# A narrow attention: the output chain of a batch one place forward in the steps, and the fill pieces one step sooner

## The chip, the cores and the metric

The kernel runs on one core of a Trainium2 chip. The metric is the device time of one execution in microseconds (us). The core has five engines that run their own instruction streams and meet only at semaphores: PE (matrix products and transpositions into PSUM), DVE (vector), ACT (activation functions and copies), POOL (general) and SP (issues transfers). Each stream runs in its written order: an instruction that waits holds up everything behind it on its engine.

## The reference, cut to what matters

Two decoder layers over `x` of 4 batches x 256 tokens x 128 channels. The change touches only the attention and the routing inside the third block ("C" in the names):

```python
# _L0_ffn_ref: attention with 16 heads of 8 channels, then a mixture of experts
q, k, v = split(h @ Wq + bq), split(h @ Wk + bk), split(h @ Wv + bv)
att = jnp.einsum('bhqd,bhkd->bhqk', q, k) / jnp.sqrt(jnp.float32(hd))
att = jax.nn.softmax(jnp.where(causal, att, -jnp.inf), axis=-1)
y = jnp.einsum('bhqk,bhkd->bhqd', att, v)
x = x + y.transpose(0, 2, 1, 3).reshape(B, T, D) @ Wp + bp
# experts: layer norm, gate logits, the two best of 8 experts for each token, weights by softmax
logits = flat @ gate_W + gate_b
top_v, top_i = jax.lax.top_k(logits, TOP_K)
mid = gelu(flat @ exp_W1[e] + exp_b1[e]); y_e = mid @ exp_W2[e] + exp_b2[e]
```

Ahead of it stand a wide self-attention (A) and a cross-attention (B) of 16 heads of 64 channels; behind it a second small attention (D), a gated product (E) and a feed-forward block (F).

## The kernel before, in words

All engines walk one list of steps written out by hand. Blocks A and B are the *wide* steps. The **narrow attention** of block C runs in steps `s` of its own (`narrow_step(s)`), from s = -3 on, of which the first few lie inside the last wide steps. A step handles one group of 4 of the 16 heads of one batch: 4 batches x 4 groups = 16 groups (`NGR`), group g = s. What a step does with a group is spread over three steps (CT = 1):

- step s: PE computes the scores of group s (L900) into the 4 banks of `ring`, after a mask product (L834) into each bank; DVE takes the row maxima (L1340, L1341, two of each, `narrow_maxima`); ACT the 8 exponentials (L639, L640), which free the banks.
- step s+1: PE transposes the probabilities in three pieces into the two banks of `ptb` (L828: pieces 0 and 1, and, behind the tail extras and the masks of the next scores, piece 2, which waits for DVE's first copy); DVE copies pieces 0 and 1 (L1377 x2), ACT piece 2 (L648).
- step s+2: PE multiplies with the values (L923, "PV"); ACT copies the product (L655).
- step s+3: PE transposes it back ("tr", L931, into `misc`); DVE divides by the sums (L1355, L1358) into `oN`.

Around this stand **extras** of a batch b, put into the lists `c_head[s]` (PE does them right after the scores, ACT ahead of the exponentials), `c_tail[s]` (PE: behind pieces 0 and 1; ACT: at the end of its step) and `c_dve[s]`. All of them, and tr, share the one PSUM bank `misc`: each use waits until the one before it has been read out (`misc_free`). They are QK and V (projections of a batch), CX (transposition of a later batch), and the *output chain* of a batch, after its last group: **OT** (transposition of `oN`, L855; evicted by ACT, L617), **OUT** (projection, L859; DVE adds bias and residual and takes layer norm statistics, L1383 to L1393; POOL the inverse deviation, L1705, L1706), **hat** (normalised rows, DVE, L1367), **X2** (their transposition, L867; ACT, L622), **GATE** (gate logits, L871; ACT, L628; then `pick` on DVE, L1223 to L1235, the two best experts), **RANK** (running counts of the picked experts, L875 to L885; ACT, L626; then `place` on DVE, L1241 to L1246, POOL's scatter of the rows to memory, and for the second batch of a half `tile_list`, L1251 to L1267). With the list SP loads the rows of the half (`tokens`).

When the scores end (group 15 in step 15) the experts begin. Their pieces stand in one list, `ORDER`: "mid:u" (PE: transposition of a tile of tokens, L954, and first product, L999; ACT: eviction L681 and gelu L688), "out:u" (second product, L1011; DVE L1439) and "put:u" (POOL scatter). `FILL` says how many of its pieces are done after each of the narrow steps 16 to 22; the rest follows after the last narrow step. The 15 tiles of the first half of the batches come first; the tokens of the second half need RANK of batch 3.

Of the kernel before, what the change touches and what calls it, by code (L numbers as in the profile page):

```python
# [32 lines left out]
P = 128  # L33
# [6 lines left out]
FILL = [(16, 1), (17, 2), (18, 2), (19, 5), (20, 6), (21, 6), (22, 3)]  # L40
# [52 lines left out]
def decoder(nc, t):  # L93
    ctx = ExitStack()
    with ctx:
# [413 lines left out]
        with nc.Block() as block:  # L509
# [83 lines left out]
            def _(act):  # L593
# [37 lines left out]
                def narrow_step(s):  # L631
                    from_narrow(c_head[s])
                    if 0 <= s < NGR:
                        if s >= PR:
                            act.wait_ge(c_pt_done, TU * (s - PR + 1))
                        for r in range(G):
                            if r % 2 == 0:
                                act.wait_ge(c_max, 2 * s + r // 2 + 1)
                            nc.scalar.activation(pr[:, s % PR, r, 0:P], ring[:, r, 0:P], ACT.Exp, bias=nmax[:, s, r:r + 1], scale=-1.0)  # L639
                            nc.scalar.activation(pr[:, s % PR, r, P:SW], ring[:, r, P:SW], ACT.Exp, bias=nmax[:, s, G + r:G + r + 1],  # L640
                                                 scale=-1.0).then_inc(c_ring_free, 1)
                    if CT <= s < NGR + CT:
# [13 lines left out]
                    from_narrow(c_tail[s])  # L656
# [536 lines left out]
            def _(dve):  # L1193
# [149 lines left out]
                def narrow_step(s):  # L1343
                    if s:
                        narrow_maxima(s)
                    for kind, b in c_head[s]:
                        if kind == "RANK":
                            place(b, misc_at[kind, b] + 1)
                    if 0 <= s - CT - 2 < NGR:
                        g = s - CT - 2  # L1350
                        b, q = g // NG, g % NG
                        prod4 = misc[:, 0:S].rearrange("p (c h v) -> p c h v", c=CB, v=VW)
                        rs = nrs[:, g, :].rearrange("p (c h) -> p c h", c=CB)
                        dve.wait_ge(misc_done, misc_at["tr", g] + 1)
                        c_ch.step(nc.vector.reciprocal(rs, prod4[:, :, :, HD]))  # L1355
                        if b >= 2 and q == 0:
                            dve.wait_ge(misc_done, misc_at["OT", b - 2] + 1)
                        nc.vector.tensor_tensor(oN[:, b % 2, :, :].rearrange("p c (h j d) -> p c h j d", j=G, d=HD)[:, :, :, q, :],  # L1358
                                                prod4[:, :, :, 0:HD], rs.unsqueeze(3).broadcast_to([P, CB, G, HD]), ALU.mult)\
                            .then_inc(misc_free, 1)  # L1360
                    for kind, b in c_dve[s]:
                        dve.wait_ge(c_rstd, b + 1)
                        if b >= 2:
                            dve.wait_ge(scattered[0], 16 * 2 * HT)
                        for c in range(CB):
                            n = 4 * (b % 2) + 2 * c
                            ins = nc.vector.tensor_scalar(hat[:, n:n + 2, 0:D], x1[:, b % 2, c, :].unsqueeze(1).broadcast_to([P, 2, D]), lmv2[:, b, c, 0:1], lrs2[:, b, c:c + 1],  # L1367
                                                          ALU.subtract, ALU.mult)
                        ins.then_inc(c_xhat, 1)
                    if CT <= s < NGR + CT:  # L1370
                        g = s - CT
                        if g >= 2:
                            dve.wait_ge(c_o_done, g - 1)
                        for u, dst in enumerate((prT[g % 2][:, :, 0, 0:P], prT[g % 2][:, 0:2, :, P:S].rearrange("p h k q -> p (h k) q"))):
                            n = TU * g + u
                            dve.wait_ge(c_pt_done, n + 1)
                            nc.vector.tensor_copy(dst, ptb[:, n % 2, :].rearrange("p (h q) -> p h q", q=P)).then_inc(c_pt_free, 1)  # L1377
                    for e in c_tail[s]:
                        kind, b = e
                        if kind == "OUT":  # L1380
# [13 lines left out]
                    for kind, b in c_head[s]:  # L1394
                        if kind == "GATE":
                            pick(b, misc_at[kind, b] + 1)
                        elif kind == "RANK" and b % 2:
                            tile_list(b // 2)
# [239 lines left out]
            def _(pool):  # L1638
# [54 lines left out]
                def narrow_step(s):  # L1693
# [8 lines left out]
                    for kind, b in c_tail[s]:  # L1702
# [149 lines left out]
```

## Time and profile before

| what | value |
|---|---|
| median of 3 runs | 649.35 us (644.24 to 649.8) |
| the profiled execution | 648.76 us |
| its span, first to last instruction | 647.0 us |
| mean granted clock of TensorE | 0.976 |
| busy: PE, DVE, ACT, POOL | 592.8, 453.6, 397.8, 199.7 us |
| narrow steps 6 to 15, maxima of step 6 to maxima of step 15 | 394.47 to 446.49 us |

All times below are of the profiled execution, counted from the start of its span. A row of the timeline gives the start, the length, the engine, the line, the operation, and in brackets how long the engine had been idle and what ended that. The rows themselves stand in a section further down.

### The profile page before, as it was taken

How to read it: one execution, taken by the hardware profiler on the slowest of the kernel's cores; microseconds unless marked ns; L12 is line 12 of the kernel's file. 1: busy time of each engine (PE TensorE's matmuls, PEld its weight loads, DVE VectorE, ACT ScalarE, POOL GpSimd, SP SyncE). 2: the span in 40 equal slices, each digit the busy share in tenths (PEclk: the TensorE clock that was granted, in tenths of full speed). 3: DMA queues.
4: the chain of work that ended last, by engine and by line, in shares of the span. 5: the costliest groups of instructions: out<-in, count | busy, mean ns of one | idle time of the engine just before them, and what ended most of it. 6: DMA issues, size and time to landing. Idle time of an engine off the chain costs nothing.

```text
span 647.0 us, 12136 instructions
## 1 busy us (share of the span) xinstructions
PE 592.8 (92%) x4082; PEld 416.4 (64%) x4082; DVE 453.6 (70%) x1343; ACT 397.8 (61%) x1234; POOL 199.7 (31%) x265
## 2 busy tenths in 40 slices
PE   5999999999999999999998899887797985899996
PEld 3667776776776766767666466565787974445543
DVE  1989787677788988999988677878332366683402
ACT  3776557777678787777676467775566762144420
POOL 1133030131442442363414523243156545101101
PEclk9999999999999999999999899999699998699999
DMA  9300990000000000000000000193544801000000
GB/s 291 124 2 13 276 59 0 2 1 2 2 1 2 2 0 2 1 2 2 1 2 2 1 2 1 50 397 121 184 164 118 305 32 49 1 0 2 16 0 18
DMA packets 39662, 36.33 MB, mean 56 GB/s; under 512 B 12496, under 2 KB 34640, under 8 KB 39216
## 3 DMA queue, kind: packets, MB, share of 16 engines
q1 hardware_dynamic: 37840, 32.33, 18.3%
q0 software_dynamic: 1472, 3.05, 1.4%
q8 instruction: 34, 0.56, 0.4%
q14 instruction: 28, 0.23, 0.1%
q10 hardware_dynamic: 288, 0.16, 0.1%
HBM read 26.39 MB, written 9.14 MB: 55 GB/s over the span
## 4 chain that ended last, share of the span: by engine, by line
PE 67%; DVE 19%; ACT 8%; issue 3%; DMA 1%; SPq 1%; POOL 0%; POOLq 0%; DVEq 0%; ACTq 0%
PE ring L1029 8%; PE ring L1078 8%; PE obank L1105 8%; PE ptb L1093 6%; PE obank L1113 5%; PE misc L1148 4%; ACT arena L755 3%; PE misc L1056 3%; DVE arena L1518 3%; PE ring L999 3%; PE ptb L1011 3%; PE misc L1057 2%; PE ring L1019 2%; DVE arena L1535 2%; DVE arena L1341 2%
## 5 line engine op out<-in xcount | busy, mean ns | idle before, releaser
L755 ACT ACTIVATE arena<-ring,arena 128x256 f32<-128x256 f32 x256 | 128.9, 519 | 4.0 <-DVE arena L1518 3.9
L1518 DVE TENSOR_REDUCE arena<-ring 128x4 f32<-128x1024 f32 x56 | 68.3, 1220 | 30.5 <-PE ring L1078 30.2
L1491 DVE COPY arena<-ptb 128x512 f32<-128x512 f32 x128 | 81.9, 681 | 2.8 <-PE ptb L1093 2.7
L1535 DVE TENSOR_SCALAR arena<-arena 128x256 f32<-128x256 f32 x256 | 82.9, 369 | 0.0
L1078 PE MATMUL ring<-arena 64*128 64x256 f32 x512 | 73.4, 406 | 0.0
L1105 PE MATMUL obank<-arena 128*64 128x256 f32 x512 | 70.3, 396 | 0.4 <-ACT arena L711 0.2
L1093 PE MATMUL ptb<-ident,arena 128*128 128x128 f32 x512 | 67.0, 274 | 0.2 <-DVE arena L1535 0.2
L1093 PEld LDWEIGHTS ptb<-ident,arena 128*128 128x128 f32 x512 | 59.0, 142 | 4.1 <-issue 0.7
L1029 PE MATMUL ring<-arena 128*128 128x512 f32 x128 | 55.8, 592 | 0.0
L1078 PEld LDWEIGHTS ring<-arena 64*128 64x128 f32 x512 | 44.6, 188 | 17.1 <-issue 10.3
L294 POOL TENSOR_TENSOR arena<-arena,const 128x2 f32<-128x2 f32 x20 | 3.8, 190 | 162.6 <-DVE arena L1212 162.6
L755 ACT ACTIVATION_READ_ACCUMULATOR arena<-ring,arena 128x1 f32 x256 | 53.0, 207 | 0.0
L1113 PE MATMUL obank<-arena 128*128 128x256 f32 x128 | 44.6, 430 | 1.0 <-ACT arena L704 1.0
L1105 PEld LDWEIGHTS obank<-arena 128*64 128x64 f32 x512 | 31.4, 137 | 20.8 <-issue 10.6
L739 ACT ACTIVATE arena<-misc,cols 128x256 f32<-128x256 f32 x32 | 15.2, 476 | 45.5 <-PE misc L1057 45.5
L1029 PEld LDWEIGHTS ring<-arena 128*128 128x128 f32 x128 | 24.2, 190 | 29.2 <-issue 28.2
L688 ACT ACTIVATE arena<-ring,arena 128x128 f32<-128x128 f32 x120 | 34.1, 371 | 10.9 <-PE ring L999 10.9
L1723 POOL DMA_INDIRECT yt<-arena x30 | 29.6, 986 | 27.9 <-DVE arena L1439 23.5
L1148 PEld LDWEIGHTS misc<-arena 128*128 128x128 f32 x256 | 33.4, 191 | 5.3 <-issue 4.2
L1756 POOL TENSOR_TENSOR arena<-arena,const 128x32 f32<-128x32 f32 x4 | 21.7, 5426 | 48.2 <-DVE arena L1483 48.2
L698 ACT ACTIVATE arena<-ring,cols 128x512 f32<-128x512 f32 x16 | 11.0, 687 | 39.7 <-PE ring L1029 39.7
L1113 PEld LDWEIGHTS obank<-arena 128*128 128x128 f32 x128 | 19.0, 188 | 25.4 <-issue 23.9
(291 smaller groups left out, 1251.5 us busy)
## 6 DMA issues: line engine op xcount, KB each, us to landing
arena<-in_M_pack_dram SPq DMA_DIRECT2D x22, 578.0 KB, 7.0
xs<-zero SPq DMA_DIRECT2D x2, 2640.0 KB, 17.1
arena<-in_F_h_dram SPq DMA_DIRECT2D x2, 1024.0 KB, 11.4
arena<-xs SPq DMA_DIRECT2D x2, 528.0 KB, 4.7
arena<-in_B_wkv_dram SPq DMA_DIRECT2D x1, 1024.0 KB, 10.1
arena<-yt SPq DMA_DIRECT2D x2, 512.0 KB, 3.7
arena<-xs SPq DMA_DIRECT2D x14, 66.0 KB, 5.4
arena<-in_F_w_dram SPq DMA_DIRECT2D x3, 256.0 KB, 12.2
```

The lines of the kernel that those rows point to most:

```text
L688: ins = nc.scalar.activation(mid[u % 3][:, hc, :], ring[:, u % 3, hc * P:(hc + 1) * P], ACT.Gelu, bias=b1[:, hc:hc + 1])
L755: ins = nc.scalar.activation(probs[g % 4][:, c, h, :], ring[:, ring_at["S", g, h] % RING, c * S:(c + 1) * S], ACT.Exp, bias=negmax[:, i, q ...
L1029: ins = nc.tensor.matmul(bank, w[:, kc, i * P:(i + 1) * P], src[:, hf, kc, :], start=kc == 0, stop=kc == FC - 1)
L1078: ins = nc.tensor.matmul(banks[h][:, c * S:(c + 1) * S], qs[rows_h, c * P:(c + 1) * P], kT[g % 2][rows_h, :], start=True, stop=True)
L1093: ins = nc.tensor.transpose(ptb[:, c, k * P:(k + 1) * P], probs[g % 4][:, c, k // 2, (k % 2) * P:(k % 2 + 1) * P], ident[:, :])
L1105: ins = nc.tensor.matmul(obank[h * A:(h + 1) * A, 0:S], vtok[bb % 2][:, kc, (2 * q + h) * A:(2 * q + h + 1) * A], probsT[g % 2][:, h, kc, ...
L1113: ins = nc.tensor.matmul(obank[:, S:2 * S], src, (A_wv if bb < B else B_wkv)[:, o:o + S], start=True, stop=True)
L1148: ins = nc.tensor.matmul(misc[:, 0:D], oT[b % 2][:, q, c * P:(c + 1) * P], wo[:, q, :], start=q % 4 == 0, stop=q % 4 == 3 and not with_null)
L1491: nc.vector.tensor_copy(probsT[g % 2][:, :, :, c * P:(c + 1) * P].rearrange("p h k q -> p (h k) q"), ptb[:, c, :].rearrange("p (k q) -> p ...
L1518: ins = nc.vector.tensor_reduce(dst[:, i1, q1, :, :].rearrange("p c h -> p h c"), ring[:, r:r + 2, :].rearrange("p h (c k) -> p h c k", c= ...
L1535: ins = nc.vector.tensor_scalar(a, a, rsum[:, i, q, k // 2, k % 2:k % 2 + 1], None, ALU.mult)
L1723: nc.gpsimd.indirect_dma_start(yt_dram[u // TILES], bass.IndirectOffsetOnAxis(unit_x(u)[:, D:D + 1].bitcast(I32), 0), ysb[:, u % YS, :], N ...
```

## The change

The places of a batch's output chain in the steps, with `end` = 4b + 7:

| | before | after |
|---|---|---|
| OT | head of `end` | tail of `end - 1` |
| OUT | tail of `end` | head of `end` |
| hat (DVE) | `end + 1`, ahead of the copies | `end`, behind the copies |
| X2 | tail of `end + 1` | head of `end + 1` |
| GATE | head of `end + 2` | tail of `end + 1` |
| RANK | head of `end + 3` | head of `end + 2` |

The narrow steps become 22 (0 to 21) instead of 23, and the pieces of `FILL` stand after the steps 15 to 21. ACT evicts an OT right behind the exponentials; DVE does OUT's sums behind the maxima and ahead of the division and the copies.

```diff
-FILL = [(16, 1), (17, 2), (18, 2), (19, 5), (20, 6), (21, 6), (22, 3)]
+FILL = [(15, 1), (16, 2), (17, 2), (18, 5), (19, 6), (20, 6), (21, 3)]
...
-        CSTEPS = NGR + CT + 6
+        CSTEPS = NGR + CT + 5
...
-            c_head[end].append(("OT", b))
-            c_tail[end].append(("OUT", b))
-            c_dve[end + 1].append(("hat", b))
-            c_tail[end + 1].append(("X2", b))
-            c_head[end + 2].append(("GATE", b))
-            c_head[end + 3].append(("RANK", b))
+            c_tail[end - 1].append(("OT", b))
+            c_head[end].append(("OUT", b))
+            c_dve[end].append(("hat", b))
+            c_head[end + 1].append(("X2", b))
+            c_tail[end + 1].append(("GATE", b))
+            c_head[end + 2].append(("RANK", b))
...
+                    from_narrow([e for e in c_tail[s] if e[0] == "OT"])
                     if CT <= s < NGR + CT:
...
-                    from_narrow(c_tail[s])
+                    from_narrow([e for e in c_tail[s] if e[0] != "OT"])
```

On DVE the block of the division, the copies, `hat` and OUT are written in the new order: maxima, `place` or OUT, division, copies, `hat`, `pick`, `tile_list`. POOL does OUT's part from `c_head`. The lines of the changed kernel are one higher from L642 on, and others where DVE's blocks were moved.

**PE, end of narrow step 6 and begin of step 7 (batch 0).** Before: tr, pieces 0 and 1, then QK of batch 2 (L845, L846), mask, piece 2, mask, scores of step 7, OT of batch 0 (L855).

```order
L931 MATMUL misc<-ident,arena 128x128 x2
L828 MATMUL ptb<-ident,arena 128x128 x8
L845 MATMUL misc<-xn_all,C_wq 128x256
L846 MATMUL misc<-xn_all,C_wk 128x256
L834 MATMUL ring<-causal,identb 128x2x128 x2
L828 MATMUL ptb<-ident,arena 128x128 x4
L834 MATMUL ring<-causal,identb 128x2x128 x2
L900 MATMUL ring<-arena 128x128 x4
L900 MATMUL ring<-arena 128x256 x4
L855 MATMUL misc<-ident,arena 128x128 x2
```

After: OT (now L856) stands between the pieces and QK (L846, L847), and OUT (L860) behind the scores.

```order
L932 MATMUL misc<-ident,arena 128x128 x2
L829 MATMUL ptb<-ident,arena 128x128 x8
L856 MATMUL misc<-ident,arena 128x128 x2
L846 MATMUL misc<-xn_all,C_wq 128x256
L847 MATMUL misc<-xn_all,C_wk 128x256
L835 MATMUL ring<-causal,identb 128x2x128 x2
L829 MATMUL ptb<-ident,arena 128x128 x4
L835 MATMUL ring<-causal,identb 128x2x128 x2
L901 MATMUL ring<-arena 128x128 x4
L901 MATMUL ring<-arena 128x256 x4
L860 MATMUL misc<-C_wp,arena 128x128 x2
```

What moved: OT of batch 0 is ahead of QK of batch 2 in one tail; the same stands in step 10 with OT of batch 1 and QK of batch 3.

**DVE, narrow steps 8 and 9 (batch 0).** Before: hat (L1367), copies of step 8, maxima of step 9, division, copies of step 9, and then `pick` (from L1223).

```order
L1367 TENSOR_SCALAR hat<-arena 128x2x128 x2
L1377 COPY arena<-ptb 128x4x128 x2
L1340 TENSOR_REDUCE arena<-ring 128x2
L1341 TENSOR_REDUCE arena<-ring 128x2
L1340 TENSOR_REDUCE arena<-ring 128x2
L1341 TENSOR_REDUCE arena<-ring 128x2
L1355 RECIPROCAL arena<-misc 128x8
L1358 TENSOR_TENSOR arena<-misc,arena 128x8x8
L1377 COPY arena<-ptb 128x4x128 x2
L1223 TENSOR_TENSOR arena<-arena,rows 128x16
```

After: copies of step 8 (L1384), the whole of `pick` (L1224 to L1236), and only then the maxima of step 9 (L1341, L1342).

```order
L1384 COPY arena<-ptb 128x4x128 x2
L1224 TENSOR_TENSOR arena<-arena,rows 128x16
L1226 MAX arena<-arena 128x8 x2
L1228 TENSOR_TENSOR arena<-arena 128x2
L1230 MAX_INDEX topi<-arena 128x8 x2
L1232 CAST arena<-topi 128x4
L1234 TENSOR_TENSOR arena<-iof,arena 128x32
L1236 TENSOR_TENSOR picked<-arena 128x16
L1341 TENSOR_REDUCE arena<-ring 128x2
L1342 TENSOR_REDUCE arena<-ring 128x2
```

What moved: `pick` stands at the end of the step in whose tail its GATE is, instead of at the end of the step in whose head it was.

**PE, the expert stream at the end of the output chain (batch 3).** Before: X2 (L867), four products, then GATE (L871).

```order
L867 MATMUL misc<-ident,hat 128x128 x2
L1011 MATMUL ptb<-arena 128x128 x8
L954 MATMUL ring<-ident,arena 128x128
L999 MATMUL ring<-arena 128x128 x4
L954 MATMUL ring<-ident,arena 128x128
L999 MATMUL ring<-arena 128x128 x4
L871 MATMUL misc<-M_gw,xn_all 128x8 x2
L1011 MATMUL ptb<-arena 128x128 x4
```

After: the same four products, then X2 (L868) and GATE (L872) next to each other.

```order
L1012 MATMUL ptb<-arena 128x128 x8
L955 MATMUL ring<-ident,arena 128x128
L1000 MATMUL ring<-arena 128x128 x4
L955 MATMUL ring<-ident,arena 128x128
L1000 MATMUL ring<-arena 128x128 x4
L868 MATMUL misc<-ident,hat 128x128 x2
L872 MATMUL misc<-M_gw,xn_all 128x8 x2
L1012 MATMUL ptb<-arena 128x128 x4
```

What moved: X2 of batch 3 goes from ahead of these pieces to behind them, where GATE follows it at once. RANK of batch 3 stands behind the same piece of the stream (mid:8) in both kernels.

## Rows read from the trace of the kernel before

**Rows 1.** Page: span, and busy time of each engine with its share

```profile
span 647.0 us, 12136 instructions
...
PE 592.8 (92%) x4082; PEld 416.4 (64%) x4082; DVE 453.6 (70%) x1343; ACT 397.8 (61%) x1234; POOL 199.7 (31%) x265
```

**Rows 2.** Timeline, DVE: first row maxima of steps 6 to 13 and 15

```profile
394.47 0.43 DVE L1340 TENSOR_REDUCE arena<-ring 128x2 f32<-128x256 f32 x1 [1.46 <-PE ring L900]
...
399.79 0.42 DVE L1340 TENSOR_REDUCE arena<-ring 128x2 f32<-128x256 f32 x1 [1.12 <-PE ring L900]
...
406.25 0.39 DVE L1340 TENSOR_REDUCE arena<-ring 128x2 f32<-128x256 f32 x1
...
411.71 0.42 DVE L1340 TENSOR_REDUCE arena<-ring 128x2 f32<-128x256 f32 x1 [1.26 <-PE ring L900]
...
417.04 0.42 DVE L1340 TENSOR_REDUCE arena<-ring 128x2 f32<-128x256 f32 x1
...
423.06 0.42 DVE L1340 TENSOR_REDUCE arena<-ring 128x2 f32<-128x256 f32 x1 [1.79 <-PE ring L900]
...
428.85 0.42 DVE L1340 TENSOR_REDUCE arena<-ring 128x2 f32<-128x256 f32 x1
...
434.27 0.42 DVE L1340 TENSOR_REDUCE arena<-ring 128x2 f32<-128x256 f32 x1 [1.26 <-PE ring L900]
...
446.49 0.42 DVE L1340 TENSOR_REDUCE arena<-ring 128x2 f32<-128x256 f32 x1
```

**Rows 3.** Timeline, step 6: QK, last exponential, scores of 7, OT's eviction in step 7

```profile
396.86 0.70 PE L845 MATMUL misc<-xn_all,C_wq 128*128 128x256 f32 x2 [0.41 <-DVE arena L1358]
...
397.67 0.52 ACT L640 ACTIVATE arena<-ring,arena 128x256 f32<-128x256 f32 x1
...
398.79 0.94 PE L900 MATMUL ring<-arena 32*128 32x128 f32 x16
...
400.81 0.47 ACT L617 ACTIVATE arena<-misc,cols 128x256 f32<-128x256 f32 x1 [0.53 <-PE misc L855]
```

**Rows 4.** Timeline, step 7, DVE: first and last of OUT's five operations

```profile
403.67 0.41 DVE L1383 TENSOR_TENSOR y<-misc,rows 128x256 f32<-128x256 f32 x1
...
405.26 0.39 DVE L1393 TENSOR_TENSOR x_res<-arena,x_res 128x256 f32<-128x256 f32 x1
```

**Rows 5.** Timeline, steps 8 and 9: V and its eviction, ACT's piece 2, begin of `pick`

```profile
404.91 0.71 PE L851 MATMUL misc<-C_wv,xn_all 128*128 128x128 f32 x4
...
405.66 0.37 ACT L615 COPY arena<-misc 128x256 f32<-128x256 f32 x1 [0.87 <-PE misc L851]
...
410.61 0.59 ACT L648 COPY arena<-ptb 128x512 f32<-128x512 f32 x1 [0.67 <-PE ptb L828]
...
415.56 0.17 DVE L1223 TENSOR_TENSOR arena<-arena,rows 128x16 f32<-128x16 f32 x1
```

**Rows 6.** Timeline, batch 3: first mid, OUT, X2, mid:5, GATE, its eviction, RANK

```profile
460.04 1.92 PE L999 MATMUL ring<-arena 128*128 128x128 f32 x8
...
470.05 0.68 PE L859 MATMUL misc<-C_wp,arena 128*128 128x128 f32 x4 [0.66 <-ACT arena L617]
...
474.53 0.41 PE L867 MATMUL misc<-ident,hat 128*128 128x128 f32 x2 [0.90 <-DVE hat L1367]
...
476.67 1.06 PE L999 MATMUL ring<-arena 128*128 128x128 f32 x8
...
478.57 0.51 PE L871 MATMUL misc<-M_gw,xn_all 128*128 128x8 f32 x4
...
480.12 0.23 ACT L628 COPY arena<-misc 128x16 f32<-128x16 f32 x1
...
482.81 0.17 PE L875 MATMUL misc<-picked,tri 128*128 128x16 bf16 x1
```

**Rows 7.** Windows of 4 us: busy PE, PEld, DVE, ACT, POOL; granted clock; DMA

```profile
448.00:452.00 4.00, 2.09 (x24) 1.55 (x24) 3.77 (x12) 3.02 (x9) 0.28 (x1) 0.95 0.12 24
...
460.00:464.00 4.00, 3.90 (x20) 3.75 (x19) 0.95 (x8) 3.32 (x8) 0.00 (x0) 0.50 0.69 218
```

More of the change, by code:

```diff
@@ L1345, in narrow_step @@
                         narrow_maxima(s)
-                    for kind, b in c_head[s]:
+                    for e in c_head[s]:
+                        kind, b = e
                         if kind == "RANK":
                             place(b, misc_at[kind, b] + 1)
[L1349 to L1377, printed above, removed]
@@ L1378, in narrow_step @@
-                    for e in c_tail[s]:
-                        kind, b = e
-                        if kind == "OUT":
+                        elif kind == "OUT":
                             dve.wait_ge(misc_done, misc_at[e] + 1)
@@ L1393, in narrow_step @@
                             nc.vector.tensor_tensor(xb, x1[:, b % 2, :, :], xb, ALU.add)
-                    for kind, b in c_head[s]:
+                    if 0 <= s - CT - 2 < NGR:
+                        g = s - CT - 2
+                        b, q = g // NG, g % NG
+                        prod4 = misc[:, 0:S].rearrange("p (c h v) -> p c h v", c=CB, v=VW)
+                        rs = nrs[:, g, :].rearrange("p (c h) -> p c h", c=CB)
+                        dve.wait_ge(misc_done, misc_at["tr", g] + 1)
+                        c_ch.step(nc.vector.reciprocal(rs, prod4[:, :, :, HD]))
+                        if b >= 2 and q == 0:
+                            dve.wait_ge(misc_done, misc_at["OT", b - 2] + 1)
+                        nc.vector.tensor_tensor(oN[:, b % 2, :, :].rearrange("p c (h j d) -> p c h j d", j=G, d=HD)[:, :, :, q, :],
+                                                prod4[:, :, :, 0:HD], rs.unsqueeze(3).broadcast_to([P, CB, G, HD]), ALU.mult)\
+                            .then_inc(misc_free, 1)
@@ new lines, in narrow_step @@
+                    for kind, b in c_dve[s]:
+                        dve.wait_ge(c_rstd, b + 1)
+                        if b >= 2:
+                            dve.wait_ge(scattered[0], 16 * 2 * HT)
+                        for c in range(CB):
+                            n = 4 * (b % 2) + 2 * c
+                            ins = nc.vector.tensor_scalar(hat[:, n:n + 2, 0:D], x1[:, b % 2, c, :].unsqueeze(1).broadcast_to([P, 2, D]), lmv2[:, b, c, 0:1], lrs2[:, b, c:c + 1],
+                                                          ALU.subtract, ALU.mult)
+                        ins.then_inc(c_xhat, 1)
@@ L1395, in narrow_step @@
+                    for kind, b in c_tail[s]:
                         if kind == "GATE":
                             pick(b, misc_at[kind, b] + 1)
-                        elif kind == "RANK" and b % 2:
+                    for kind, b in c_head[s]:
+                        if kind == "RANK" and b % 2:
                             tile_list(b // 2)
@@ L1701, in narrow_step @@
                                                     gmask[:, j:j + 2].unsqueeze(2).broadcast_to([P, 2, S]), ALU.mult).then_inc(kz_pool, 1)
-                    for kind, b in c_tail[s]:
+                    for kind, b in c_head[s]:
                         if kind == "OUT":
```

8 lines of the change are left out of this document (added).

## The prediction

> **What bounds the kernel now.** I read the page first. PE is busy for 92% of the span, DVE for 70% [rows 1], but shares over the whole span say little about a change that moves work in 80 us of it. So I went to the timeline of the narrow steps and looked at one event in each: the first row maxima on DVE. They mark the beat of the loop, since the next scores need the ring banks that the exponentials free, and the exponentials need the maxima. Nine steps, 6 to 15, take 446.49 - 394.47 = 52.02 us, 5.78 in the mean [rows 2]. No engine is full in such a step. The loop is: maxima, exponentials and copies, piece 2 and masks, scores, maxima. Five of the rows show DVE free and waiting for the scores by 1.1 to 1.8 us [rows 2]; in the others DVE came from other work. A wait put into this loop lengthens the step, unless it lies beside the exponentials.
>
> Behind step 15 the beat is that of PE's expert stream. Its first mid starts at 460.04, RANK of batch 3 stands at 482.81 [rows 6], and from there on the stream is the same in both kernels. So two distances decide: maxima 6 to maxima 15 (52.02), and maxima 15 to RANK of batch 3 (482.81 - 446.49 = 36.32) [rows 2, 6].
>
> **The loop, step by step.** Nothing is added or removed; no DMA is added, and SP's list is the same. Batch 0 has its chain in steps 6 to 9, batch 1 in 10 to 13.
>
> *Steps 6 and 10: OT ahead of QK.* Before, QK started at 396.86 and nothing waited behind it until the scores at 398.79. Now QK must wait until ACT has evicted OT, and ACT does that behind its exponentials, which end at 397.67 + 0.52 = 398.19. With 0.47 for the eviction QK starts at about 398.65, 1.8 later, and masks, piece 2 and scores are queued behind it [rows 3]. **+1.8** in step 6. In step 10 the same, less what `place` no longer does there: four small operations, which I estimate at 0.65 from the 1.48 that `pick` takes with ten (415.56 to 417.04) [rows 2, 5]. **+1.15**. Lower bound of both: 0.4 each, if ACT's exponentials ended where QK started.
>
> *Steps 7 and 11: OUT ahead of the copies.* OUT on DVE runs from 403.67 to 405.26 + 0.39, that is 1.98 [rows 4]. Before, it lay behind the copies, partly under the next scores (0.94 [rows 3]). Now the first copy, and with it piece 2 and the scores, come 1.98 later. In step 7 DVE was already the limit (its maxima 8 came straight from other work, with no idle time in the row [rows 2]); the order costs nothing there, but hat joins the step: two operations, estimated at 2 x 0.39 from OUT's last. **+0.7**. In step 11, 1.98 less the 0.94 that covered it: **+1.05**. Bounds 0 and 2 each.
>
> *Steps 8 and 12: V behind X2, and `pick` ahead of the next maxima.* V shares bank and head with X2 now. ACT's head holds both evictions ahead of the exponentials: X2 0.41 [rows 6], its eviction about 0.47 as OT's [rows 3], V 0.71 and 0.37 [rows 5] make 1.96 behind the scores, while the maxima that the exponentials also need take about one. The exponentials come 0.9 later, of which piece 2's own chain hides half. That is +0.3 in step 8 (where DVE is late anyway) and +0.5 in step 12. The larger part is `pick`. It needs GATE's logits, evicted at the end of ACT's step, behind piece 2's copy (0.59 [rows 5]), PV's copy (about V's 0.37) and 0.2 of its own: 1.2 behind piece 2. Masks and scores also take about 1.1 there. So `pick`, 1.48, stands on DVE exactly where the maxima could start. Before, it ran while PE still made the scores: it ended at 417.04, and that was no later than the scores allowed [rows 2, 5]. **+1.8 and +2.0**. RANK's product on PE then waits for `pick` at a head, with PV and tr behind it; but DVE is busy with maxima and `place` then, so that is free. Lower bound 0.3 each, if the logits came before the copies end.
>
> *Steps 9, 13 and 14.* `place` comes one step sooner: +0.2 in step 9. `tile_list` moves with RANK from 14 to 13; the two steps had 446.49 - 434.27 = 12.22 together [rows 2] and hold the same work: 0.
>
> Sum of the loop: 1.8 + 0.7 + 1.8 + 0.2 + 1.15 + 1.05 + 2.0 + 0 = **+8.7 us** (bounds 1.5 and 12).
>
> **The tail.** Before, 460.04 - 446.49 = 13.55 lie between maxima 15 and the first mid [rows 2, 6]. The fill now goes in ahead of the last PV and tr, half a step sooner: half of 5.78, -2.9. But OUT of batch 2 lies ahead of step 15's copies: +1.98. Then from first mid to RANK, 22.77 [rows 6]: PE's waits at OUT (0.66) and at X2 (0.90) go [rows 6], since other work now stands there. Two come: OT directly behind the last tr waits for DVE's division, estimated at 0.6; and GATE directly behind X2 waits until ACT is through with the gelu of mid 6. How late ACT is there, the rows show: PE was at GATE at 478.57, ACT at its eviction at 480.12, 1.55 later [rows 6]; with X2's own eviction (0.47) less PE's X2 that is about 1.8. Sum: -2.9 + 1.98 - 0.66 - 0.90 + 0.6 + 1.8 = -0.08, **0** (bounds -3 and +3). The wait for the second half's tokens stays: RANK of batch 3 has the same place in the stream, and everything from it to the tokens is queued as before.
>
> **The clock.** In the window 448 to 452 PE was busy for 2.09 of 4 us, and the mean granted clock of that window is 0.95, so it fell at its end; in 460 to 464 it was 0.50, 1.2 instead of 2.4 GHz [rows 7]. The eight passes of a mid took 1.92 there and 1.06 later at full clock [rows 6]. The sum above assumes that the tail has the same share at half clock. The Trainium skill, "TensorE: Matmul & The Clock Gate", section "Part 1: The HAM clock gate", says that the throttled state is the default and only recent activity lifts it; the trace agrees with the 0.95 and 0.50 above. By that rule longer steps with the same PE work speak against this change, and the time would be that of the third rival below.
>
> **Sum.** 648.76 (the profiled execution, 1.76 above its span, 0.59 below the median 649.35) + 8.7 + 0 = 657.46: **657.5 us**.
>
> **The rivals.**
> 1. *The loop does not lengthen.* Place: the handing over from exponentials to scores in steps 6 to 14. If the exponentials end later than every wait that I add, all of it lies beside them. For it: in five rows DVE waits for PE anyway [rows 2]. Against: QK's new wait begins when they end, and `pick` stands behind them on DVE. It decides from the point where OT's eviction and GATE's logits are there before piece 2. Then +8.7 becomes about 0: 648.8, no change. Chance 0.20.
> 2. *A whole step is saved.* The loop as in 1, and the stream starts a full step sooner without the new waits at OT and GATE: -5.78, 643.0, faster. Against it: X2 and GATE of batch 3 next to each other on PE. Chance 0.08.
> 3. *The clock falls inside the longer steps too.* Steps 7, 11 and 15 now have PE waiting for DVE's OUT, about 2 us each. Work of PE on the loop per step is at most scores 0.94 [rows 3] and about as much for piece 2 and masks; at half clock up to +1.8 in each of three steps: 657.5 + 5.4 = 662.9. For it: the fall at the end of 448 to 452 [rows 7]. Against: the windows that I looked at between step 6 and 448 show no fall. Chance 0.14.
>
> **How the numbers follow.** Forecast 0.58, rivals 0.20, 0.08, 0.14. The likeliest case has its own range, 653 to 663, from the estimated terms. The range 647 to 664 takes in the first and third rival and leaves out the second and the far ends. One per cent, about what a measurement of this kernel can tell from no change, is 6.5 us: faster is below 642.9, slower above 655.8. Slower: 0.7 of the forecast and all of the third rival, 0.41 + 0.14 = 0.55. Faster: 0.08. The same: 0.37.
>
> **What would show it.** In the profile after: QK starting right behind OT's eviction on ACT, some 1.8 us behind its DVE release; `pick` directly ahead of maxima 9 and 13, these starting about 1.5 behind the end of the scores; maxima 6 to 15 in about 60.7 us instead of 52.0; PE idle for 1.5 to 2 us between X2 and GATE of batch 3; RANK of batch 3 about 36 behind maxima 15; everything behind it shifted, not changed. The prediction is wrong if the nine steps take less than 55 us, or if RANK of batch 3 comes 33 or less behind maxima 15.

## The result, and the profile after

The changed kernel takes 654.53 us in the median of 4 runs (651.38 to 656.28), the kernel before beside it 648.08 us (4 runs): ratio **1.0108**, 95% interval 1.0074 to 1.0143. A second measurement gave 656.71 against 646.41 us, ratio **1.0151**, 1.0119 to 1.0184. The change costs 1.1 to 1.5%. The profiled execution took 656.28 us, 7.52 more than that of before.

The page of the profile after, span and busy time, beside [rows 1]:

```profile
span 654.5 us, 12136 instructions
...
PE 592.8 (91%) x4082; PEld 415.5 (63%) x4082; DVE 453.4 (69%) x1343; ACT 397.8 (61%) x1234; POOL 199.6 (30%) x265
```

The same instructions with the same busy times in a span 7.5 us longer: in sum, all of it is waiting. The timeline of DVE shows where, with the first row maxima of steps 6 to 15, beside [rows 2]:

```profile
394.86 0.42 DVE L1341 TENSOR_REDUCE arena<-ring 128x2 f32<-128x256 f32 x1 [1.47 <-PE ring L901]
...
401.92 0.42 DVE L1341 TENSOR_REDUCE arena<-ring 128x2 f32<-128x256 f32 x1 [2.88 <-PE ring L901]
...
408.76 0.42 DVE L1341 TENSOR_REDUCE arena<-ring 128x2 f32<-128x256 f32 x1
...
416.02 0.41 DVE L1341 TENSOR_REDUCE arena<-ring 128x2 f32<-128x256 f32 x1
...
421.52 0.42 DVE L1341 TENSOR_REDUCE arena<-ring 128x2 f32<-128x256 f32 x1 [1.26 <-PE ring L901]
...
428.58 0.42 DVE L1341 TENSOR_REDUCE arena<-ring 128x2 f32<-128x256 f32 x1 [3.55 <-PE ring L901]
...
435.42 0.42 DVE L1341 TENSOR_REDUCE arena<-ring 128x2 f32<-128x256 f32 x1 [0.62 <-PE ring L901]
...
442.68 0.41 DVE L1341 TENSOR_REDUCE arena<-ring 128x2 f32<-128x256 f32 x1
...
449.57 0.42 DVE L1341 TENSOR_REDUCE arena<-ring 128x2 f32<-128x256 f32 x1
...
455.87 0.42 DVE L1341 TENSOR_REDUCE arena<-ring 128x2 f32<-128x256 f32 x1 [2.79 <-PE ring L901]
```

The nine steps take 455.87 - 394.86 = 61.01 us, 8.99 more than before (52.02 [rows 2]). Two of the causes stand in the timelines of PE and ACT. Step 6: ACT evicts OT at 398.42, and QK, idle for 1.26, begins as this ends; before, QK began at 396.86 [rows 3].

```profile
398.42 0.53 ACT L617 ACTIVATE arena<-misc,cols 128x256 f32<-128x256 f32 x1
...
398.99 0.70 PE L846 MATMUL misc<-xn_all,C_wq 128*128 128x256 f32 x2 [1.26 <-ACT arena L617]
...
400.93 0.94 PE L901 MATMUL ring<-arena 32*128 32x128 f32 x16
```

Step 8: the scores of step 9 begin at 413.68 and are through by 414.62, but DVE has been waiting for GATE's logits since its copies, starts `pick` at 414.54, and so comes to the maxima at 416.02.

```profile
413.68 0.94 PE L901 MATMUL ring<-arena 32*128 32x128 f32 x16
...
414.54 0.18 DVE L1224 TENSOR_TENSOR arena<-arena,rows 128x16 f32<-128x16 f32 x1 [1.12 <-ACT arena L628]
```

The tail, on PE: first mid, OT, GATE and RANK of batch 3, and the first tile of the second half, beside [rows 6].

```profile
468.52 1.06 PE L1000 MATMUL ring<-arena 128*128 128x128 f32 x8
...
476.40 0.41 PE L856 MATMUL misc<-ident,arena 128*128 128x128 f32 x2 [0.65 <-DVE arena L1374]
...
486.11 0.79 PE L872 MATMUL misc<-M_gw,xn_all 128*128 128x8 f32 x4 [1.73 <-ACT xn_all L622]
...
492.05 0.17 PE L876 MATMUL misc<-picked,tri 128*128 128x16 bf16 x1
...
505.44 0.30 PE L955 MATMUL ring<-ident,arena 128*128 128x128 f32 x1 [1.23 <-DMA arena<-xs]
```

RANK of batch 3 stands 492.05 - 455.87 = 36.18 behind maxima 15; before it was 36.32. So the tail as a whole took the same time, but not in the same way. The windows from maxima 15 to RANK, the kernel before first, give the length, PE's busy time, and as third number from the end the granted clock:

```profile
446.49:482.81 36.32, 28.88 (x218) 26.29 (x216) 16.54 (x70) 20.87 (x63) 11.25 (x14) 0.81 0.48 161
...
455.87:492.05 36.18, 27.77 (x234) 24.56 (x235) 16.62 (x69) 20.66 (x63) 11.01 (x14) 0.91 0.45 156
```

PE's waits in the tail, as the timeline lists them, sum to 8.40 instead of 7.44, about 1 us more, and a granted clock of 0.91 instead of 0.81 gave back as much in its busy time (27.77 instead of 28.88). Behind RANK 1.7 us came back, of which 1.10 lie at the second half's tokens; the row of the kernel before for the same place is

```profile
497.30 0.30 PE L954 MATMUL ring<-ident,arena 128*128 128x128 f32 x1 [2.33 <-DMA arena<-xs]
```

The account of the span: +0.39 ahead of maxima 6, +8.99 in the nine steps, -0.14 in the tail, -1.10 at the tokens, and the rest, 7.5 - 8.14 = -0.6, in the blocks behind.

### The profile page after: what moved, and what is told of

Same layout as the page of the kernel before. It is cut to its first block, busy times and chain, and to the rows that moved or that the text cites. A ratio compares the mean times of both kernels' runs of the same rounds, so it can differ in the third digit from the quotient of the medians.

```text
span 654.5 us, 12136 instructions
## 1 busy us (share of the span) xinstructions
PE 592.8 (91%) x4082; PEld 415.5 (63%) x4082; DVE 453.4 (69%) x1343; ACT 397.8 (61%) x1234; POOL 199.6 (30%) x265
## 4 chain that ended last, share of the span: by engine, by line
PE 68%; DVE 18%; ACT 9%; issue 3%; DMA 1%; SPq 1%; POOL 0%; POOLq 0%; DVEq 0%; ACTq 0%
PE ring L1030 8%; PE ring L1079 8%; PE obank L1106 8%; PE ptb L1094 6%; PE obank L1114 5%; PE misc L1149 4%; ACT arena L756 3%; PE misc L1057 3%; PE ptb L1012 3%; DVE arena L1519 3%; PE ring L1000 2%; PE misc L1058 2%; DVE arena L1342 2%; PE ring L1020 2%; PE ring L1124 2%
```

## The experiments

Because a step is bounded by first maxima, the trace of one execution prices each step. Every row below is one profiled execution. Lengths in us, from the first maxima of a step to those of the next; 52.02 and 61.01 are the sums for the two kernels of the study. **Bold**: TensorE's granted clock fell to half inside that step.

| kernel | 5 | 6 | 7 | 8 | 9 | 10 | 11 | 12 | 13 | 14 | 6 to 14 |
|---|---|---|---|---|---|---|---|---|---|---|---|
| before | 4.98 | 5.32 | 6.46 | 5.46 | 5.33 | 6.02 | 5.79 | 5.42 | 5.33 | 6.89 | 52.02 |
| changed | 4.99 | 7.06 | 6.84 | 7.26 | 5.50 | 7.06 | 6.84 | 7.26 | 6.89 | **6.30** | 61.01 |
| OT moved alone | 4.99 | 7.06 | 6.02 | 5.46 | 5.32 | 7.09 | 5.34 | 5.42 | 5.32 | 6.89 | 53.92 |
| changed, QK away | 5.32 | 4.98 | 7.25 | 7.26 | 6.04 | 4.98 | 6.68 | 7.27 | **6.89** | 4.97 | 56.32 |
| changed, logits first | 4.98 | 7.06 | 6.82 | 6.17 | 5.50 | 7.06 | 6.84 | 6.16 | 6.89 | **5.57** | 58.07 |
| changed, list late | 4.98 | **8.69** | 6.69 | 7.27 | 5.50 | 7.06 | 6.83 | 7.27 | 5.50 | 4.98 | 59.79 |
| changed, all three | 5.31 | 4.98 | 7.26 | 6.17 | 6.03 | 4.98 | 6.69 | 6.17 | 5.49 | 4.99 | 52.76 |
| changed, once more | 4.98 | **8.46** | 6.68 | 7.27 | 5.49 | **8.69** | 6.69 | 7.27 | 6.89 | **6.28** | 63.72 |
| before, list late | 4.99 | 5.31 | 6.46 | 5.47 | 5.32 | 6.03 | 5.80 | 5.41 | 5.33 | 5.50 | 50.63 |
| batch 3 alone | 4.98 | 5.31 | 6.47 | **6.03** | **7.14** | 6.04 | 5.79 | 5.42 | 5.32 | 6.90 | 54.42 |
| tuned | 4.98 | 5.31 | 6.47 | **5.99** | **7.19** | 6.04 | 5.79 | 5.42 | 5.32 | 5.50 | 53.03 |
| tuned, QK away | 5.31 | 4.98 | 6.02 | 5.47 | 6.35 | 5.50 | 5.91 | 5.42 | 5.32 | 5.50 | 50.47 |

The theory was that three added waits lengthen the loop: QK behind OT's eviction (steps 6, 10), OUT ahead of the copies (7, 11), `pick` ahead of the next maxima (8, 12). The rivals: that the later half of the chain does it and OT is hidden, or that the clock does it.

### OT moved alone

The kernel before with one row of the change, and ACT's eviction of OT behind the exponentials as in the change:

```diff
-            c_head[end].append(("OT", b))
+            c_tail[end - 1].append(("OT", b))
```

> The kernel before with one move only: the output transposition OT of every batch goes one place forward, into the tail of the step, ahead of QK, and ScalarE evicts it right behind the exponentials; projection, rows, gates, ranks and the fill stay where they were. Theory (three added waits lengthen the loop, one of them QK behind OT's eviction): steps 6 and 10 take 1.7 us more each (7.0 and 7.7 instead of 5.3 and 6.0), the others stay; with some 0.7 us for OT behind the last division at the end of the attention the time is 3.5 to 4.5 us longer, ratio to before 1.005 to 1.007. Rival A (the loss belongs to the later half of the chain, OUT ahead of the copies, pick ahead of the maxima, and OT is hidden): steps 6 and 10 within 0.3 us of before, ratio 1.000 to 1.001. Rival B (the loss is the clock, which falls elsewhere): no step longer where the granted clock is full, the ratio anything between 0.997 and 1.004.

Measured: 648.62 us, ratio 1.0020 (0.9999 to 1.0041). Step 6 is 7.06, exactly as in the changed kernel, and QK's row reads the same:

```profile
397.02 0.70 PE L846 MATMUL misc<-xn_all,C_wq 128*128 128x256 f32 x2 [1.26 <-ACT arena L617]
```

So the wait is OT's, and rival A falls: step 6 lost 1.74 with OT alone. The time as a whole rose by less than was expected (1.005 to 1.007), and its interval touches no change. My size was too large, in two places. Step 10 is 7.09, not 7.7: `place`, which here is still in step 10, adds nothing, since it lies beside OT's wait. And steps 7 and 11 became 0.44 and 0.45 shorter, as OT no longer stands at their head. The nine steps cost 1.90, not 3.4 (twice 1.7).

### QK taken out of OT's step

```diff
-                (c_head[5] if b == 2 else c_tail[9]).append(("CX", b))
-            c_tail[-1 if b == 1 else s0 - 2].append(("QK", b))
+                (c_head[5] if b == 2 else c_head[9]).append(("CX", b))
+            c_tail[-1 if b == 1 else s0 - 2 if b == 0 else s0 - 3].append(("QK", b))
```

> The changed kernel with QK of batches 2 and 3 taken out of OT's step: QK goes from the tails of steps 6 and 10 into those of 5 and 9, and the transposition of the context of batch 3 from the tail of step 9 to its head. Theory: the wait of QK for OT's eviction goes, steps 6 and 10 fall back from 7.06 to about 5.3 each, and steps 5 and 9 grow by at most 0.5 each; 2.0 to 3.3 us less than the changed kernel, so a ratio to before of 1.006 to 1.008. Rival A (later half of the chain): no more than 0.5 us less, ratio to before 1.010 to 1.011. Rival B (clock): steps 6 and 10 stay as they are in the changed kernel, ratio 1.007 to 1.014 without a pattern.

Measured: 650.64 us, ratio 1.0043 (1.0018 to 1.0068). Behind OT the mask now starts at once:

```profile
395.74 0.41 PE L856 MATMUL misc<-ident,arena 128*128 128x128 f32 x2 [0.47 <-DVE arena L1374]
395.99 0.38 PE L835 MATMUL ring<-causal,identb 128*128 128x256 bf16 x2
```

Steps 6 and 10 fall by 2.08 each, to 4.98; steps 5, 7 and 9 take back 0.33, 0.41 and 0.54, and step 11 gives 0.16. The net for QK is 3.0, inside the expected 2.0 to 3.3. The ratio came out below the expected 1.006 to 1.008, since the nine steps gained 1.33 more in step 14, which is not QK's: at full clock that step is 4.97, in the changed kernel, at half clock, 6.30. The fall in step 13 cost nothing: at half clock it takes the same 6.89 as at full clock in the changed kernel.

### The logits evicted first

ACT takes GATE, like OT, behind the exponentials, in place of behind its two copies.

```diff
-                    from_narrow([e for e in c_tail[s] if e[0] == "OT"])
+                    from_narrow([e for e in c_tail[s] if e[0] in ("OT", "GATE")])
...
-                    from_narrow([e for e in c_tail[s] if e[0] != "OT"])
+                    from_narrow([e for e in c_tail[s] if e[0] not in ("OT", "GATE")])
```

> The changed kernel, but ScalarE evicts the logits of GATE right behind its exponentials, ahead of its copies of piece 2 and of the product with V, in place of behind them. Nothing else moves. Theory (pick stands ahead of the next maxima because its logits come late): in steps 8 and 12 pick starts about 1.0 us sooner, at the end of VectorE's copies, the maxima of steps 9 and 13 come 0.8 to 1.1 us sooner, and the time falls by 1.6 to 2.2 us against the changed kernel: ratio to before 1.007 to 1.008. Rival A (pick is not on the path; steps 8 and 12 are long because V stands behind X2, which holds the exponentials back): steps 8 and 12 stay at 7.26 within 0.3, ratio 1.010 to 1.011. Rival B (ScalarE is the limit there, and piece 2's copy just comes 0.2 later): steps 0.2 longer.

Measured: 652.42 us, ratio 1.0064 (1.0037 to 1.0090). In the timeline of step 8 ACT evicts at 413.57, `pick` follows DVE's copies without a gap, and the maxima come at its end:

```profile
413.57 0.23 ACT L628 COPY arena<-misc 128x16 f32<-128x16 f32 x1
...
413.83 0.17 DVE L1224 TENSOR_TENSOR arena<-arena,rows 128x16 f32<-128x16 f32 x1
...
414.08 0.94 PE L901 MATMUL ring<-arena 32*128 32x128 f32 x16
...
415.32 0.42 DVE L1341 TENSOR_REDUCE arena<-ring 128x2 f32<-128x256 f32 x1
```

Steps 8 and 12 fall by 1.09 and 1.10. Of the 1.80 and 1.84 that they lost, that much was the late logits. What the other 0.7 is, step 8 shows. The scores of step 9 end here at 415.02, 5.87 behind maxima 8 (409.15); in the kernel before they end at 411.66, 5.41 behind (406.25 [rows 2]):

```profile
410.72 0.94 PE L900 MATMUL ring<-arena 32*128 32x128 f32 x16
```

So 0.46 are later scores, as the exponentials now stand behind the evictions of X2 and V, and 0.30 are the end of `pick`, for which DVE still makes the maxima wait. The nine steps gained 0.73 more in step 14, which ran at half clock for a shorter part; that is not the logits'. The ratio, 1.0064, lies just under the expected 1.007 to 1.008.

### The tile list later

SP loads the tokens of the first half ahead of its wait for the list; DVE makes the list where no maxima follow:

```diff
-                        if kind == "RANK" and b % 2:
-                            tile_list(b // 2)
+                        if kind == "RANK" and b == 3:
+                            tile_list(b // 2)
+                    if s == NGR:
+                        tile_list(0)
```

> The changed kernel with one piece of VectorE's work moved: the tile list of the first half goes from the end of step 13, where the maxima of step 14 follow it directly, to the end of step 16, where no more maxima come; SyncE loads the first half's tokens ahead of its wait for that list. Theory (the 0.97 us that steps 13 and 14 lost against the kernel before come from the tile list and from what it makes late, OT of batch 2, which waited 1.86 us): step 13 falls from 6.89 to about 5.5, step 14 keeps its 6.3 or falls to 5.6 where the clock stays up, together 1.3 to 2.1 us less, ratio to before 1.007 to 1.009. Rival A (the list lies beside work of TensorE): steps 13 and 14 still 13.2 together, ratio 1.010 to 1.011. Rival B (the list is needed early: the weights of the listed tiles come later and TensorE waits for them): the steps are shorter, but a new wait for the listed tiles' loads stands in the expert stream, ratio 1.010 or more.

Measured: 652.50 us, ratio 1.0076 (1.0050 to 1.0103), as expected. Its step 6 ran partly at half clock (8.69), so its sum of nine steps is not to be compared; steps 13 and 14 are. Step 13 is 5.50 instead of 6.89, since the maxima of step 14 now wait for PE's scores and not for DVE:

```profile
445.40 1.28 DVE L1384 COPY arena<-ptb 128x512 f32<-128x512 f32 x2
447.94 0.42 DVE L1341 TENSOR_REDUCE arena<-ring 128x2 f32<-128x256 f32 x1 [1.26 <-PE ring L901]
```

Step 14 is 4.98, at full clock. In the changed kernel OT of batch 2 began 2.46 behind maxima 14 (452.03), here 2.47 (450.41): the 1.86 that PE waited there were no loss of their own. The 1.3 between 6.30 and 4.98 come behind OT, at half clock, in this window of the changed kernel:

```profile
452.00:456.00 4.00, 3.97 (x28) 2.79 (x29) 1.22 (x3) 2.50 (x8) 0.00 (x0) 0.57 0.28 59
```

The same edit in **the kernel before**:

> The kernel before with the same move of the tile list alone, from the end of step 14 to the end of step 16, and the tokens' load ahead of the wait for it. Theory: step 14 falls from 6.89 to about 5.4, no other step changes, ratio to before 0.997 to 0.999. Rival A (step 14 is bound elsewhere): 6.9 stays, ratio 1.000. Rival B (listed tiles late): a wait in the expert stream, ratio 1.001 or more.

Measured: 644.59 us, ratio 0.9958 (0.9934 to 0.9982). Step 14 falls from 6.89 to 5.50, no other step moves; SP's loads of the listed tiles bring no new wait to PE's stream. The list had cost the kernel before 1.39 too, in step 14 instead of 13. The time fell by 2.8 us; what the half beyond the step comes from is not shown: the tail of the profiled execution, 34.78 instead of 36.32, had a granted clock of 0.90 instead of 0.81.

### All three

> The changed kernel with the three edits together: QK of batches 2 and 3 out of OT's step, the logits evicted right behind the exponentials, the tile list at the end of step 16. What is left of the change in the loop is OUT ahead of the copies (steps 7 and 11) and V behind X2 (part of steps 8 and 12). Theory (the waits add up, each in its own steps): 61.0 us from maxima 6 to 15 fall by 3.0 for QK, 2.2 for the logits and 1.4 for the list, to about 54.4, still 2.4 over the kernel before; with the first half of the run 0.3 longer and the tail as in the changed kernel the ratio to before is 1.001 to 1.004. Rival (they hide one another, and taking one away brings the next to light): maxima 6 to 15 stay above 56.5, ratio 1.005 or more.

Measured: 646.37 us, ratio 0.9978 (0.9957 to 0.9998), under the expected 1.001 to 1.004; 52.76 from maxima 6 to 15. The three edits take 8.25 of 61.01: 3.36 in steps 6, 7, 9, 10 and 11, 2.18 in 8 and 12, 2.71 in 13 and 14. Each is what it was alone, so they add up, and the rival falls. It came out below the 54.4 because the list's edit was worth 2.7 with step 14 at full clock. With the waits gone the change brings nothing beyond the kernel before with the list's edit alone (0.9958): the intervals overlap, and the nine steps are still 2.13 longer (52.76 against 50.63).

### Batch 3 alone

Batches 0 to 2 as before, batch 3 and `FILL` as in the change (`if b == 3:` with the new six rows, `else:` with the old).

> The kernel before with only batch 3 moved as in the changed kernel (OT, OUT, hat, X2, GATE and RANK of batch 3 one place forward, the fill one step sooner); batches 0 to 2 as before. Theory (the loss is all in the loop of the first three chains, and the tail by itself gains): maxima 6 to 15 take 52.0 us as before; behind maxima 15 the fill saves half a step (2.9 us) and two waits (0.66 and 0.90), and the waits of OT and of GATE behind X2 cost 0.6 and 1.7; with that 2.1 us less than before, ratio 0.996 to 0.998. Rival (the tail itself pays for the sooner fill, the gain is lost to the waits of RANK and GATE of batch 3 or to the tokens): ratio 1.000 to 1.003.

Measured: 646.85 us, ratio 0.9988 (0.9963 to 1.0013): not told from no change; neither the expected 0.996 to 0.998 nor the rival's 1.000 to 1.003 is ruled out. In its profile the first mid stands 10.45 behind maxima 15, where it was 13.55, so the sooner fill moved the first mid by the 2.9 (3.10). But RANK of batch 3 came only 0.63 sooner. The windows from first mid to RANK, the kernel before first, show why:

```profile
460.04:482.81 22.77, 19.86 (x146) 19.36 (x145) 7.55 (x40) 15.04 (x46) 9.32 (x11) 0.81 0.63 224
...
459.19:484.43 25.24, 21.41 (x167) 20.14 (x167) 8.38 (x45) 15.57 (x48) 9.93 (x12) 0.88 0.60 209
```

PE has 1.55 more work there, at a higher clock: what the fill overtook now stands behind the first mid. And its waits are 3.83 instead of 2.91. The two largest are X2 (L876 in this kernel) waiting for `hat`, GATE (L880) for X2's eviction:

```profile
PE misc L876 <- DVE hat L1375: 1.5, 1, 1.5
PE misc L880 <- ACT xn_all L630: 0.7, 1, 0.7
```

`hat` waited 2.38 for POOL, where the scatters of batch 2 and the stores of the first pieces were queued ahead of the inverse deviation:

```profile
476.45 0.74 DVE L1375 TENSOR_SCALAR hat<-arena 128x256 f32<-128x256 f32 x2 [2.38 <-POOL arena L1725]
```

Over the whole tail PE waited 8.46, where it was 7.44, so the sooner fill saved no waiting. The nine steps were expected to stay at 52.0 and are 2.4 longer although nothing is changed there: the clock fell in steps 8 and 9.

### Tuned

From these: batch 3 as in the run above up to X2, two output pieces between X2 and GATE, the stores of pieces behind the rows on POOL, fewer pieces ahead of X2 (14 of the list instead of 16), and the list's edit. Ahead of RANK stand 22 pieces, as in the other kernels. The lines that set batch 3 and the pieces (the other batches stand as in the kernel before):

```diff
+            if b == 3:
+                c_tail[end - 1].append(("OT", b))
+                c_head[end].append(("OUT", b))
+                c_dve[end].append(("hat", b))
+                c_head[end + 1].append(("X2", b))
+                c_head[end + 2].append(("GATE", b))
+                c_head[end + 3].append(("RANK", b))
...
+FILL = [(15, 1), (16, 2), (17, 2), (18, 3), (19, 6), (20, 4), (21, 4), (22, 3)]
...
+ "gate:0 mid:0 mid:1 mid:2 out:0 mid:3 out:1 mid:4 out:2 out:3 mid:5 put:0 put:1 mid:6 out:4 out:5 put:2 put:3 mid:7 mid:8 put:4 put:5 "
```

> Batches 0 to 2 as in the kernel before, batch 3 one place forward up to X2, its GATE and RANK at the kernel before's steps but with fewer pieces of the fill ahead of them, two output pieces between X2 and GATE, the stores of the first pieces behind the rows of batch 3 on GpSimd, and the tile list of the first half at the end of step 16. Theory: step 14 is 1.5 us shorter; the two waits ahead of X2 (1.50) and GATE (0.75) of batch 3, which the kernel with only batch 3 moved showed, go; the wait for the second half's tokens (0.97 there) shrinks; against the kernel before 3.5 to 6.5 us less, ratio 0.990 to 0.995. Rival (the end of the chain is set by ScalarE's queue and GpSimd's scatters, not by TensorE's order): RANK of batch 3 still 35.5 or more behind maxima 15, only the list's 1.5 us are gained, ratio 0.996 to 0.999.

Measured: 640.89 us, ratio **0.9900** (0.9870 to 0.9930), the lowest ratio of all, under both kernels and, narrowly, under the kernel before with the list's edit alone (0.9934 to 0.9982). First mid, X2, GATE and RANK of batch 3 on PE, none of the last three with a wait ahead of it:

```profile
456.31 1.06 PE L1008 MATMUL ring<-arena 128*128 128x128 f32 x8
...
472.87 0.41 PE L876 MATMUL misc<-ident,hat 128*128 128x128 f32 x2
...
475.01 0.58 PE L880 MATMUL misc<-M_gw,xn_all 128*128 128x8 f32 x4
...
477.65 0.17 PE L884 MATMUL misc<-picked,tri 128*128 128x16 bf16 x1
...
491.14 0.30 PE L963 MATMUL ring<-ident,arena 128*128 128x128 f32 x1 [1.11 <-DMA arena<-xs]
```

RANK stands 31.69 behind maxima 15 (445.96); before 36.32. PE's waits make 1.35 of these 4.63 (6.09 in sum instead of 7.44). The work ahead of RANK is the same, so the rest goes with the clock, which was full in the whole stretch, where the kernel before had 0.81 in the mean and ran its first mids at half (1.92 [rows 6] against 1.06). Both tuned kernels kept the full clock there in their profiled execution, and none of the ten others did; whether the order does that was not tested. In the loop 2.4 us were lost to a fall in steps 8 and 9. A last run moved QK to steps 5 and 9 in this kernel:

> The kernel tuned (batches 0 to 2 as before, batch 3 sooner, its pieces and the first tile list moved) with QK of batches 2 and 3 in steps 5 and 9 in place of 6 and 10, and the context's transposition of batch 3 at the head of step 9. Theory: without OT in QK's step there is no wait to be saved, QK only changes its step: steps 6 and 10 fall by 0.33 and up to 1.0, steps 5 and 9 grow by 0.33 and up to 0.7; ratio to before 0.989 to 0.991, no change against tuned. Rival (any extra product in the loop costs its own length, and in steps 5 and 9 it is covered): 1.0 to 1.5 us less than tuned, ratio 0.987 to 0.989.

Measured: 642.07 us, ratio 0.9924 (0.9896 to 0.9952), no gain: the intervals overlap, and the ratio is a little above the expected 0.989 to 0.991. Step 6 fell to 4.98, and step 5 rose to 5.31; step 10 fell by 0.52, but step 9 rose by 1.02, more than the expected 0.7 (against the kernel before). At full clock the nine steps take 50.47, against 50.63 in the kernel before with the list's edit: without OT in its step QK has no wait to lose.

### The changed kernel once more

> The changed kernel itself, not altered, as the measure for the other runs. Theory (the loop costs 9.0 us, and the 1.7 that the first profile gave back behind RANK of batch 3 are the tokens' landing and the place of the clock's falls): the steps 6 to 12 take the same times to within 0.05 us as in the first profile wherever the granted clock is full, and 61.0 from maxima 6 to 15 with at most 2 us of difference where it is not; ratio to before 1.009 to 1.013. Rival (the first profile was one of many and the steps differ from run to run): steps differ by 0.3 or more at full clock.

Measured: 656.71 us, ratio 1.0151 (1.0119 to 1.0184), above the expected 1.009 to 1.013, and the nine steps differ by 2.71, where at most 2 were expected. Steps 8, 9, 12, 13 and 14 repeat to 0.02 us. Steps 7 and 11 come out 0.16 and 0.15 shorter, both directly behind a step that ran at half clock. Steps 6 and 10 do not repeat: 8.46 and 8.69 in place of 7.06. QK's wait is the same (1.25 in both steps), and the windows that hold the end of these steps show the cause, a granted clock of 0.57 and 0.62:

```profile
400.00:404.00 4.00, 4.00 (x30) 2.75 (x28) 0.49 (x2) 1.60 (x4) 2.73 (x4) 0.57 0.00 0
...
428.00:432.00 4.00, 3.98 (x29) 2.75 (x28) 0.36 (x2) 1.60 (x4) 0.38 (x1) 0.62 1.01 408
```

So the steps are fixed by the waits, and the clock comes on top of them, in some executions.

## Why the prediction was right, step by step

- **The two distances that decide.** Right in size: +8.99 and -0.14 against +8.7 and 0, but both in part by luck. The seven terms of the loop came to 8.02 in sum, 0.68 less than the 8.7; steps 13 and 14 added 0.97, which was not in the sum. In the tail, more waiting was offset by a higher clock. The time, 654.53 and 656.71 in two measurements against 657.5, lies in the forecast's own range.
- **Steps 6 and 10, OT ahead of QK.** Predicted +1.8 and +1.15, measured +1.74 and +1.04; QK began 398.99 - 394.86 = 4.13 behind maxima 6 and before 2.39 [rows 2, 3], 1.74 later, where 1.8 were worked out. The mechanism is shown by the first two experiments. The reason given for the smaller term of step 10 (the four operations of `place`, priced from `pick`'s ten, which are nine in the program) was wrong: not `place` leaving, but that OT's wait fixes the step at 7.1 with `place` or without, and step 10 was already 0.70 longer than step 6 before.
- **Steps 7 and 11, OUT ahead of the copies.** Predicted +0.7 and +1.05, measured +0.38 and +1.05. The sum hid two terms: moving OT out of these heads gives back 0.44 and 0.45, which I did not price, and OUT with `hat` then costs 0.82 and 1.50 (6.84 against 6.02 and 5.34 in the kernel with OT moved alone). So the exact hit in step 11 is luck, two errors that cancel.
- **Steps 8 and 12, `pick` ahead of the maxima.** Predicted +1.8 and +2.0, measured +1.80 and +1.84; the maxima of step 9 came 1.40 behind the end of the scores, 1.5 were forecast. That the late logits are the larger part was right: 1.09 and 1.10. V behind X2 was priced at 0.3 in step 8, and the scores came 0.46 later.
- **Step 9.** +0.17 against +0.2.
- **Steps 13 and 14.** Here the sum failed: 0 was predicted, "they hold the same work", and 0.97 was measured. The list did cost the same in either step, 1.39 (two experiments). With the list late and at full clock the two steps take 10.48 in the changed kernel (5.50 + 4.98) and 10.83 in the kernel before (5.33 + 5.50), so the order costs nothing here. What cost is step 14: OT of batch 2 is in its tail, and its end ran at half clock, +1.3. I had left the third OT out of the loop because no QK stands behind it, and that was right for the wait, not for the clock.
- **The tail.** The number was met, the account only in part. First mid 12.65 behind maxima 15 against 13.55, -0.90; the terms gave -2.9 + 1.98 = -0.92. From there to RANK 23.53 against 22.77, +0.76; the terms gave -0.66 - 0.90 + 0.6 + 1.8 = +0.84, and the waits are in the rows, 0.65 at OT and 1.73 at GATE. (The 1.8 was mis-added: 1.55 + 0.47 - 0.41 is 1.6.) Two steps of this sum did not hold. It took the same share at half clock, and that was 0.81 before and 0.91 after in the mean. And it counted the fill's 2.9 as time saved up to RANK, but batch 3 alone shows that the sooner fill moves the first mid (3.10) and hardly RANK (0.63), as the work that it overtakes then stands behind the first mid. PE waited about 1 us more in the tail, and the clock gave that back.
- **"Everything behind it shifted, not changed".** Not quite: 1.7 came back. The tokens landed 13.39 behind RANK instead of 14.49, with SP's load issued 8.93 behind RANK in both. The kernel before with the late list shows 14.50 and all the others 13.1 to 13.5. Why the landing differs stays open.
- **The rivals.** Rival 1 (no longer loop) and 2 (a step saved) are out. Rival 3 (the clock inside the longer steps) was given 0.14 and does occur, but in other steps than named: in 14 in both profiled executions of the changed kernel, by 1.3 us, and in 6 and 10, behind QK's wait, by 1.4 and 1.6 us in one execution and not in the other. I had priced it at 1.8 a step in 7, 11 and 15. So of the first profile's 8.99 some 1.3 are the clock's, and the second's 63.72 is 2.71 above the first; the other 7.7 stand at full clock.

## What to carry to other kernels

Where one PSUM bank serves several users in order, moving one of them forward puts the next behind its eviction, and that stands behind whatever the evicting engine has queued: look at that engine's row, not at the moved instruction's length. In a loop with a beat, price every step apart from its first event, before and after: an instruction leaving a step gives time back, and two waits in one step do not add. One profile is enough where neither the step nor the one ahead of it ran at half clock: such steps repeat to 0.02 us. Before a whole stretch is called unchanged, compare the granted clock in it as well. Here it hid about 1 us of added waiting. The order that lengthens the loop for three batches need not be thrown away for the last one, behind the loop: where the waits that it brings were filled with other work, PE waited 6.09 in the tail instead of 7.44.

## What the runs showed of the hardware

The clock's falls are not at fixed places of the program. The kernel with batch 3 alone, and the tuned one, have the same instructions in steps 8 and 9 as the kernel before, and there theirs fell to 0.50 in the window 412 to 416 and cost 2.4 us, while the kernel before had 1.00. Step 0 lies ahead of everything that the change moves: from its first maxima to those of step 1 it took 9.5 us in five of the twelve profiled executions, at 1.00 throughout, and 11.0 to 11.1 in the other seven, whose clock was 0.50 in the window 364 to 366. The same 1.25 us wait of QK was followed by a fall in one execution of the changed kernel and by none in the other, whose windows 396 to 404 show 1.00. Over the four executions of the first measurement the changed kernel's span goes with the mean granted clock: 654.5 us at 0.976 (twice), 651.1 at 0.983, 649.6 at 0.986. That is a spread of 4.9 us, against an effect of 6.5 to 10.3. In the second it runs from 652.3 us at 0.981 to 657.4 at 0.971, but 653.3, 654.9 and 655.0 stand at one 0.976. The Trainium skill, "TensorE: Matmul & The Clock Gate", section "HAM oscillation — how this bites in real kernels", describes a product stream that waits for transfers between bursts and is throttled each time. The rows here agree that falls follow waits: in each of the nine falls that the table marks, PE had waited 1.25 to 1.86 us shortly before. They add that a given wait brings a fall only in some executions. What decides in which was not settled.
